# Four clears of the accumulator in flight at most, and the rows of x for the second stage fetched one per step

## The chip, the core and the metric

The kernel is one program on one core of a Trainium2 chip. The metric is the device time of one execution in microseconds (us). The engines named below are PE (matrix multiply), DVE (vector), ACT (scalar functions), POOL (GpSimd; here it issues the indirect DMAs and, in the second stage, normalizes) and SP (here it only issues plain DMAs). Each takes its own instructions in order and meets the others at semaphores. DMAs issued by SP, ACT and POOL run on the same 16 DMA engines.

## What is computed

One layer of a message-passing network over 50,000 atoms and 50,000 edges with 256 features, then a layer norm over 2x + m:

```python
h = x @ W_in2f
Wij = ssp(rbf @ Wf1 + bf1) @ Wf2 + bf2      # ssp(z) = softplus(z) - log 2
Wij = Wij * dist_cut
x_ij = h[idx_j] * Wij
m = jax.ops.segment_sum(x_ij, idx_i, num_segments=n_atoms)
m = ssp(m @ Wo1 + bo1) @ Wo2 + bo2
return x + m
...
x = _layernorm(x + _L0_gnn_ref(...), axis=-1)
```

## The kernel before

**Stage one** goes over the edges in G = 98 groups of 512 (R = 4 rows of 128 edges in each). POOL gathers the rows of x that the edges name (line 341, four gathers of 128 rows a group, into the ring `xg` of XRING = 11 groups). PE turns them (420), multiplies by W_in2f (409) and makes the filter from `attr`; ACT and DVE evaluate softplus and split each operand into a high and a low part; PE multiplies the message by Wo1 at once, sums edges of a group that go to the same atom (495), and ACT copies the result into `sums`, a ring of RING = 12 groups. POOL adds `sums` into the accumulator `acc` in HBM with four indirect scatter-adds a group (354). Every engine runs its stages with lags: in step s, PE turns and filters group s, multiplies group s-1, and so on to group s-3; DVE's `compare` (744), last in its step, handles group s-2.

**The accumulator is cleared first.** `acc` has 50,512 rows of 256 floats. SP fills them with `fill` (a constant row) in 195 DMAs of 256 KB (line 271) and three more for the rest (279), all on one semaphore `cleared`. The first scatter waits for all of them. SP's order is written out by hand: eight clears (EARLY_CLEARS), a wait until group 0 is gathered, clears up to number 36 (FIRST_CLEARS), the three of the rest, and then for n = 2 to 98: `load_attr(n)` (250, two DMAs, waits for a freed buffer through `al_sb`), `load_src(n-1)` (255, waits for `compare` of group n-3 through `same_ready`), and 16 more clears (CLEARS_A_STEP) as long as there are any. The last 15 stand behind `load_src(10)`.

**POOL's order** is written out too: 23 groups are gathered first (AHEAD; from group 11 on each waits until PE has turned group g-11), then come the scatters of one group and three or four gathers in turn. The first scatter of a group waits until those of the group before have landed (`added`).

**Stage two** goes over the atoms in 98 groups of 512: SP fetches rows of `acc` (`fetch_m`, 293) and of x (`fetch_x`, 299), PE turns and multiplies by Wo2, and POOL normalizes (379 to 385); SP stores (304). The x rows use the ring `xg` again, 11 groups. The first 11 x fetches stand in SP's order behind all loads of stage one, in a burst; each waits until PE has turned the last edge group in its slot (`xt_ps`). The first `fetch_m` waits until all scatters have landed.

Of the kernel before, what the change touches and what calls it, by code (L numbers as in the profile page):

```python
# [44 lines left out]
P = 128  # L45
R = 4
RING = 12
XRING = 11
ARING = 2
SRING = 2  # L50
AHEAD = 23
EARLY_CLEARS = 8
FIRST_CLEARS = 36
CLEARS_A_STEP = 16
LOG2 = 0.6931471805599453
LN_MAX = 40.0
# [17 lines left out]
def wait(eng, sem, value):  # L74

    if isinstance(value, int) and value <= 0:
        return
    eng.wait_ge(sem, value)  # L78


def build(nc, t, out):
    N, D = t["x"].shape
    E = N
    G, A = t["edge_attr_64"].shape[:2]
# [5 lines left out]
    def group(n):  # L90
        return Group(n, n % 2, n // 2 + 1, ROWS if n < G - 1 else TAIL)

    def run(*stages, before={}):

        for s in range(G + max(lag for _, lag in stages)):
            if s in before:
                before[s]()  # L100
            for stage, lag in stages:
                if 0 <= s - lag < G:
                    stage(group(s - lag))

    acc = nc.dram_tensor("acc", [N + R * P, D], F32, kind="Internal").ap()

    with ExitStack() as ctx:
        def sb(name, shape, dt=F32):
            return ctx.enter_context(nc.sbuf_tensor(name, shape, dt))

        def sem(name):
            return ctx.enter_context(nc.semaphore(name))
# [31 lines left out]
        CLEAR = 2  # L144
        fill = sb("fill", [P, CLEAR, D])
# [26 lines left out]
        x_in = xg  # L172
# [6 lines left out]

        dve_own = sem("dve_own")  # L180
        dst_in, src_in, wgt_in, tab_made = sem("dst_in"), sem("src_in"), sem("wgt_in"), sem("tab_made")
        bo1_in, fill_made, cleared = sem("bo1_in"), sem("fill_made"), sem("cleared")
        made = sem("made")
        bo2_zero, bo2_in = sem("bo2_zero"), sem("bo2_in")
        wf1_in, w_in_in, b_in, wf2_in, wo1_in, wo2_in = (sem(n) for n in ("wf1_in", "w_in_in", "b_in", "wf2_in", "wo1_in", "wo2_in"))
# [6 lines left out]
        xg_in = [sem(f"xg_in{u}") for u in range(XRING)]  # L192
# [4 lines left out]
        xt_ps = sem("xt_ps")  # L197
# [16 lines left out]
        x_got = [sem(f"x_got{u}") for u in range(XRING)]  # L214
# [3 lines left out]
        res_sb, mean_sb = sem("res_sb"), sem("mean_sb")  # L218
# [4 lines left out]

        block = ctx.enter_context(nc.Block())

        CLEARS = N // P // CLEAR
        TABLES = 1 + R
        assert N // P % CLEAR == 0
        CLEAR_REST = len(range(CLEARS * CLEAR * P, N + R * P, CLEAR * P))

        def rows_of(ap, g):

            return ap[bass.ds(g.n * ROWS, g.rows)]
# [9 lines left out]
        @block.sync  # L243
        def _(sp):

            def load_attr(n):
                g, u = group(n), n % ARING
                wait(sp, al_sb, n - ARING + 1)
                for k in range(2):
                    sp.dma_start(attr[k * A:(k + 1) * A, u], t["edge_attr_64"][n]).then_inc(attr_in[u], 16)  # L250

            def load_src(n):
                g, u = group(n), n % SRING
                wait(sp, same_ready, (n - SRING + 1) * R)
                sp.dma_start(srcb[:, u], t["src_rows"][n].partition_broadcast(P)).then_inc(srcb_in[u], 16)

            sp.dma_start(dst_t[:].rearrange("p r g -> p (r g)"), t["dst"].rearrange("p r g -> p (r g)")).then_inc(dst_in, 16)
            load_attr(0)
            sp.dma_start(bo1, t["L0_gnn_bo1"].partition_broadcast(P)).then_inc(bo1_in, 16)
            sp.dma_start(src_i.rearrange("p r g -> p (r g)"), t["src"].rearrange("p r g -> p (r g)")).then_inc(src_in, 16)  # L260
            sp.dma_start(wgt_t[:].rearrange("p r g -> p (r g)"), t["edge_weight1"].rearrange("p r g -> p (r g)")).then_inc(wgt_in, 16)
            load_attr(1)
            load_src(0)

            sp.wait_ge(fill_made, 1)
            clears = 0

            def clear_to(count):
                nonlocal clears
                for c in range(clears, min(count, CLEARS)):  # L270
                    sp.dma_start(acc[c * CLEAR * P:(c + 1) * CLEAR * P, :].rearrange("(p k) d -> p (k d)", k=CLEAR), fill[:, 0:CLEAR].rearrange("p k d -> p (k d)")).then_inc(cleared, 16)
                clears = max(clears, min(count, CLEARS))

            clear_to(EARLY_CLEARS)
            sp.wait_ge(xg_in[0], 16 * R)
            clear_to(FIRST_CLEARS)
            for a in range(CLEARS * CLEAR * P, N + R * P, CLEAR * P):
                b = min(a + CLEAR * P, N + R * P)
                sp.dma_start(acc[a:b, :].rearrange("(p k) d -> p (k d)", k=CLEAR), fill[0:(b - a) // CLEAR].rearrange("p k d -> p (k d)")).then_inc(cleared, 16)
            for n in range(2, G + 1):  # L280
                if n < G:
                    load_attr(n)
                load_src(n - 1)
                clear_to(FIRST_CLEARS + (n - 1) * CLEARS_A_STEP)
            assert clears == CLEARS
            wait(sp, al_sb, G - ARING + 1)
            sp.dma_start(wo2, t["L0_gnn_Wo2"]).then_inc(wo2_in, 16)

            def fetch_m(g):
                if g.n == 0:  # L290
                    sp.wait_ge(added, 16 * R * G)
                wait(sp, mt_ps, (g.n - MRING + 1) * H)
                sp.dma_start(m_in[0:g.p, g.n % MRING].rearrange("p r d -> p (r d)"), rows_of(acc, g).rearrange("(p r) d -> p (r d)", r=R)).then_inc(m_got[g.n % MRING], 16)

            def fetch_x(g):
                if g.n < XRING:
                    sp.wait_ge(xt_ps, 2 * max(n + 1 for n in range(G) if n % XRING == g.xs))
                wait(sp, res_sb, g.n - XRING + 1)
                sp.dma_start(x_in[0:g.p, g.xs].rearrange("p r d -> p (r d)"), rows_of(t["x"], g).rearrange("(p r) d -> p (r d)", r=R)).then_inc(x_got[g.xs], 16)

            def store(g):
                u = g.n % NRING
                sp.wait_ge(norm_sb, g.n + 1)
                sp.dma_start(rows_of(out, g).rearrange("(p r) d -> p (r d)", r=R), normed[0:g.p, u].rearrange("p r d -> p (r d)")).then_inc(stored[u], 16)

            for n in range(G - XRING, G):
                fetch_x(group(n % XRING))
            for s in range(G + 8):
                if s < G:
                    fetch_m(group(s))  # L310
                if 8 <= s:
                    store(group(s - 8))
                if XRING <= s - 1 < G:
                    fetch_x(group(s - 1))

            for u in range(NRING):
                sp.wait_ge(stored[u], 16 * len(range(u, G, NRING)))
# [3 lines left out]
        def _(pool):  # L321
# [23 lines left out]
            def scatter(r):  # L345
                def stage(g):
                    if r == 0:
                        if g.n == 0:
                            pool.wait_ge(cleared, 16 * (CLEARS + CLEAR_REST))
                        pool.wait_ge(src_ready, g.n + 1)  # L350
                        wait(pool, added, g.n * R * 16)
                    if r % 2 == 0:
                        pool.wait_ge(y_sb, g.n * 2 + r // 2 + 1)
                    pool.indirect_dma_start(acc, bass.IndirectOffsetOnAxis(ap=src_ix[g.slot][0:g.p, r:r + 1], axis=0),  # L354
                                            sums[0:g.p, g.slot, r], None, compute_op=ALU.add).then_inc(added, 16)
                return stage
# [526 lines left out]
```

## Time and profile before

| | |
|---|---|
| median of 3 runs | 1865.61 us (1861.05 to 1866.87) |
| the profiled execution | 1858.28 us, span 1856.5 us |
| granted PE clock, mean of the span | 0.972 |
| busy share of the span | PE 91%, PEld 83%, DVE 80%, ACT 80%, POOL 78% |
| DMA | 363.47 MB, 196 GB/s over the span |
| queue q1 (SP's DMAs) | 257.75 MB |
| queue q0 (POOL's DMAs) | 102.45 MB |

A busy share is a mean over stages that have different limits; the 40 slices of the page show three of them: a start with idle engines and full DMA, the long stage one with DMA at six or seven tenths, and stage two with DMA nearly full. POOL's share leaves out the time in which it issues, some 0.3 us in front of each indirect DMA.

### The profile page before, as it was taken

To read this page: it belongs to the slowest core of one execution; us is meant where nothing else is said; L and a number is where in the kernel's file an instruction comes from. 1 tells how busy PE (TensorE), PEld (TensorE's weight loads), DVE (VectorE), ACT (ScalarE), POOL (GpSimd) and SP (SyncE) were. 2 spreads that over 40 slices of the span, in tenths; PEclk is the share of its full clock that TensorE was granted. 3 is DMA by queue.
4 is the path that set the end of the run, shared out by engine and by line. 5 is a ranking of instruction groups with operands and counts; after the bars stand their busy time and mean duration, and the time that the engine had idled before them with its cause. 6 is when DMAs were issued, how large, how long until landed. Compare 5 with 4: busy or idle time off the path is not lost. (4 is left out here: it accounts for less than half of the span.)

```text
span 1856.5 us, 36676 instructions
## 1 busy us (share of the span) xinstructions
PE 1697.3 (91%) x11376; PEld 1532.2 (83%) x11376; DVE 1489.3 (80%) x3750; ACT 1492.9 (80%) x2945; POOL 1441.4 (78%) x1385
## 2 busy tenths in 40 slices
PE   3499899999999999999999998889976999999995
PEld 2378788888888888888888887778866999999995
DVE  2477788787888888888888786777765999999996
ACT  2477788778888788888888786776756999999996
POOL 7422488888887888878888888888754999999997
PEclk9699999999999999999999998999998999999998
DMA  9799866656566665666665666665675999999994
GB/s 354 251 356 372 266 123 112 126 112 125 115 125 122 112 123 114 124 125 112 125 120 116 119 122 113 114 118 108 116 185 170 333 363 362 360 360 364 357 366 174
DMA packets 177341, 363.47 MB, mean 196 GB/s; under 512 B 25622, under 2 KB 76264, under 8 KB 177148
## 3 DMA queue, kind: packets, MB, share of 16 engines
q1 hardware_dynamic: 101128, 257.75, 39.8%
q0 software_dynamic: 75136, 102.45, 32.4%
q8 instruction: 93, 1.52, 0.3%
q10 hardware_dynamic: 884, 0.92, 0.2%
q14 instruction: 100, 0.82, 0.1%
HBM read 206.90 MB, written 154.12 MB: 194 GB/s over the span
## 5 line engine op out<-in xcount | busy, mean ns | idle before, releaser
L354 POOL DMA_INDIRECT acc<-sums,src_ix x392 | 637.2, 1626 | 141.6 <-issue 116.0
L341 POOL DMA_INDIRECT xg<-in_x,dst_t x392 | 401.4, 1024 | 215.6 <-issue 114.6
L780 DVE SCALAR_TENSOR_TENSOR m_l<-pair,wgt_t,m_h 128x256 fp32r<-128x256 f32 x392 | 171.6, 479 | 230.5 <-ACT m_h L621 206.6
L385 POOL TENSOR_SCALAR sums<-sums,neg_mean,rstd 128x256 f32<-128x256 f32 x392 | 283.2, 733 | 10.2
L495 PE MATMUL pair<-m_h,same 128*128 128x256 f32 (+1 forms) x980 | 244.8, 285 | 30.4 <-ACT sums L628 21.9
L621 ACT ACTIVATE m_h<-pair,wgt_t 128x256 fp32r<-128x256 f32 x392 | 165.0, 475 | 99.5 <-PE pair L409 57.6
L495 PE MATMUL pair<-m_l,same 128*128 128x256 f32 (+1 forms) x980 | 241.8, 281 | 0.0
L409 PE MATMUL pair<-wo_h,msg_h 128*128 128x256 f32 (+1 forms) x784 | 230.9, 295 | 6.0 <-DVE m_l L780 5.2
L495 PEld LDWEIGHTS pair<-m_h,same 128*128 128x128 f32 (+1 forms) x980 | 185.1, 189 | 52.2 <-issue 34.9
L576 ACT ACTIVATE zs<-pair,bf 128x512 f32<-128x512 f32 x196 | 124.1, 685 | 125.8 <-PE pair L433 99.5
L409 PE MATMUL pair<-wo_h,msg_l 128*128 128x256 f32 (+1 forms) x784 | 222.0, 283 | 0.0
L409 PE MATMUL pair<-wo_l,msg_h 128*128 128x256 f32 (+1 forms) x784 | 221.5, 283 | 0.0
L527 PE MATMUL pair<-w_in_l,ssp_h 128*128 128x256 f32 (+1 forms) x784 | 220.6, 281 | 0.0
L527 PE MATMUL pair<-w_in_h,ssp_l 128*128 128x256 f32 (+1 forms) x784 | 220.5, 281 | 0.0
L527 PE MATMUL pair<-w_in_h,ssp_h 128*128 128x256 f32 (+1 forms) x784 | 220.3, 281 | 0.0
L744 DVE SCALAR_TENSOR_TENSOR same<-srcb,src_t,later 128x512 fp32r<-128x512 int32 (+3 forms) x392 | 192.8, 546 | 0.0
L495 PEld LDWEIGHTS pair<-m_l,same 128*128 128x128 f32 (+1 forms) x980 | 185.0, 189 | 6.7
L763 DVE SCALAR_TENSOR_TENSOR msg<-pair,bias_w,h_sb 128x512 f32<-128x512 f32 x196 | 146.1, 746 | 54.7 <-remote 37.6
L673 DVE TENSOR_TENSOR ssp_l<-ssp,ssp_h 128x512 fp32r<-128x512 f32 (+1 forms) x245 | 186.2, 793 | 4.5 <-ACT ssp_h L653 2.8
L409 PE MATMUL pair<-ssp_h,wf_h 128*128 128x512 f32 x392 | 164.4, 419 | 25.8 <-DVE msg L763 25.8
L409 PE MATMUL pair<-x_h,w_in_h 128*128 128x512 f32 x392 | 155.5, 397 | 18.7 <-issue 18.6
L662 ACT ACTIVATE srcb<-sums,neg_mean 128x256 f32<-128x256 f32 x294 | 158.9, 636 | 3.1 <-DVE neg_mean L835 3.1
(97 smaller groups left out, 5249.8 us busy)
## 6 DMA issues: line engine op xcount, KB each, us to landing
acc<-fill SPq DMA_DIRECT2D x197, 256.0 KB
xg<-in_x SPq DMA_DIRECT2D x97, 512.0 KB, 6.4
sums<-acc SPq DMA_DIRECT2D x97, 512.0 KB, 6.8
out<-sums SPq DMA_DIRECT2D x97, 512.0 KB, 4.7
attr<-in_edge_attr SPq DMA_DIRECT2D x196, 128.0 KB
srcb<-in_src_rows SPq DMA_DIRECT2D x98, 256.0 KB
xg<-in_x,dst_t POOLq DMA_INDIRECT x392
acc<-sums,src_ix POOLq DMA_INDIRECT x392
```

The costliest lines, as they stand in the source:

```text
L341: pool.indirect_dma_start(xg[0:g.p, g.xs, r], None, t["x"], bass.IndirectOffsetOnAxis(ap=dst_t[0:g.p, r, g.n:g.n + 1], axis=0)).then_inc(x ...
L354: pool.indirect_dma_start(acc, bass.IndirectOffsetOnAxis(ap=src_ix[g.slot][0:g.p, r:r + 1], axis=0), sums[0:g.p, g.slot, r], None, compute ...
L385: last = pool.tensor_scalar(normed[0:g.p, g.n % NRING, r], res[0:g.p, u, r], neg_mean[0:g.p, u, r:r + 1], rstd[0:g.p, u, r:r + 1], ALU.add ...
L409: last = pe.matmul(o, a, b, start=n == 0, stop=n == len(terms) - 1)
L495: last = pe.matmul(o, same[0:g.p, g.par, FROM[a] + b - a, 0:g.p], m[0:g.p, a], start=a == 0 and m is m_h, stop=a == b and m is m_l)
L527: last = pe.matmul(o, sp2[:, g.par, h, r, 0:g.p], w[:, h, :], start=False, stop=h == H - 1 and sp2 is ssp2_l)
L621: act.activation(m_h[0:g.p, r], bank[6][0:g.p, k * D:(k + 1) * D], ACT.Copy, scale=col(wgt_t, r, g)).then_inc(mh_sb, 1)
L662: last = act.activation(squares[0:g.p, r], res[0:g.p, u, r], ACT.Square, bias=neg_mean[0:g.p, u, r:r + 1], accum_out=square[0:g.p, u, r:r ...
L673: dve.tensor_tensor(out_, whole, high.bitcast(F32), ALU.subtract).then_inc(done, count)
L744: dve.scalar_tensor_tensor(out=same[0:g.p, g.par, FROM[a]:FROM[a] + R - a, 0:g.p], in0=sources[:, a:R], scalar=col(src_t, a, g), in1=later ...
L763: dve.scalar_tensor_tensor(out=msg[:, m], in0=bank[5][:], scalar=bias_w[:, m:m + 1], in1=h_sb[:, m], op0=ALU.add, op1=ALU.mult).then_inc(m ...
L780: dve.scalar_tensor_tensor(out=m_l[0:g.p, r], in0=bank[6][0:g.p, k * D:(k + 1) * D], scalar=col(wgt_t, r, g), in1=m_h[0:g.p, r].bitcast(F3 ...
```

## The change

Clears now use four semaphores in turn, and before clear c is issued SP waits until clear c-4 has landed. The wait for group 0 after eight clears is gone. The rest of the rows is no longer cleared early: it is part of the count, which becomes 198, so that the last two clears stand one step later, behind `load_src(11)`. POOL's first scatter waits on the four semaphores. `fetch_x` is called once per step for n = 89 to 98, behind that step's `load_src`, and once behind the loop; before, all 11 stood behind the loop.

```diff
-EARLY_CLEARS = 8
 FIRST_CLEARS = 36
+IN_FLIGHT = 4
...
-        bo1_in, fill_made, cleared = sem("bo1_in"), sem("fill_made"), sem("cleared")
+        bo1_in, fill_made = sem("bo1_in"), sem("fill_made")
+        cleared = [sem(f"cleared{u}") for u in range(IN_FLIGHT)]
...
-        CLEARS = N // P // CLEAR
+        CLEARS = -(-(N + R * P) // (P * CLEAR))
...
                 for c in range(clears, min(count, CLEARS)):
-                    sp.dma_start(acc[c * CLEAR * P:(c + 1) * CLEAR * P, :]...).then_inc(cleared, 16)
+                    a, b = c * CLEAR * P, min((c + 1) * CLEAR * P, N + R * P)
+                    wait(sp, cleared[c % IN_FLIGHT], c // IN_FLIGHT * 16)
+                    sp.dma_start(acc[a:b, :]...).then_inc(cleared[c % IN_FLIGHT], 16)
                 clears = max(clears, min(count, CLEARS))
 
-            clear_to(EARLY_CLEARS)
-            sp.wait_ge(xg_in[0], 16 * R)
             clear_to(FIRST_CLEARS)
-            for a in range(CLEARS * CLEAR * P, N + R * P, CLEAR * P):
...
                 clear_to(FIRST_CLEARS + (n - 1) * CLEARS_A_STEP)
+                if G - XRING <= n - 2:
+                    fetch_x(group((n - 2) % XRING))
...
-            for n in range(G - XRING, G):
+            for n in range(G - 1, G):
                 fetch_x(group(n % XRING))
...
                         if g.n == 0:
-                            pool.wait_ge(cleared, 16 * (CLEARS + CLEAR_REST))
+                            for u in range(IN_FLIGHT):
+                                pool.wait_ge(cleared[u], 16 * len(range(u, CLEARS, IN_FLIGHT)))
```

SP at the start of the program, before (`acc<-fill` is a clear, `fill_made` says that the constant row is there, `xg_in0` that group 0 is gathered):

```order
8 L271 DMA acc<-fill 128x512 [waits fill_made]
9 L271 DMA acc<-fill 128x512 x7
10 L271 DMA acc<-fill 128x512 [waits xg_in0]
11 L271 DMA acc<-fill 128x512 x27
12 L279 DMA acc<-fill 128x512 x2
13 L279 DMA acc<-fill 40x512
14 L250 DMA attr<-in_edge_attr 64x512 [waits al_sb]
```

and in the changed kernel, where rows 10 to 41 are 32 clears with a wait each:

```order
8 L273 DMA acc<-fill 128x512 [waits fill_made]
9 L273 DMA acc<-fill 128x512 x3
10 L273 DMA acc<-fill 128x512 [waits cleared0]
11 L273 DMA acc<-fill 128x512 [waits cleared1]
...
41 L273 DMA acc<-fill 128x512 [waits cleared3]
42 L250 DMA attr<-in_edge_attr 64x512 [waits al_sb]
```

Each clear from the fifth on has moved behind the landing of the one four places ahead, and the wait for group 0 has gone.

SP at the end of the clears, before (the last 15, then two steps' loads) and in the changed kernel:

```order
52 L255 DMA srcb<-in_src_rows 128x512 [waits same_ready]
53 L271 DMA acc<-fill 128x512 x15
54 L250 DMA attr<-in_edge_attr 64x512 [waits al_sb]
55 L250 DMA attr<-in_edge_attr 64x512
56 L255 DMA srcb<-in_src_rows 128x512 [waits same_ready]
```

```order
232 L250 DMA attr<-in_edge_attr 64x512 [waits al_sb]
233 L250 DMA attr<-in_edge_attr 64x512
234 L255 DMA srcb<-in_src_rows 128x512 [waits same_ready]
235 L273 DMA acc<-fill 128x512 [waits cleared0]
236 L273 DMA acc<-fill 40x512 [waits cleared1]
```

The row with 40 partitions, once at the start, now ends the clears, behind the `load_src` that waits for one group more.

SP at the end of stage one, before and in the changed kernel (`xg<-in_x` is a fetch of x, 512 KB):

```order
311 L255 DMA srcb<-in_src_rows 128x512 [waits same_ready] x2
312 L287 DMA attr<-in_L_gnn_Wo 128x512 [waits al_sb]
313 L299 DMA xg<-in_x 128x1024 [waits xt_ps] x11
314 L293 DMA sums<-acc 128x1024 [waits added]
```

```order
499 L255 DMA srcb<-in_src_rows 128x512 [waits same_ready]
500 L282 DMA xg<-in_x 128x1024 [waits xt_ps]
501 L255 DMA srcb<-in_src_rows 128x512 [waits same_ready]
502 L282 DMA xg<-in_x 128x1024 [waits xt_ps]
503 L293 DMA attr<-in_L_gnn_Wo 128x512 [waits al_sb]
504 L282 DMA xg<-in_x 128x1024 [waits xt_ps]
505 L299 DMA sums<-acc 128x1024 [waits added]
```

Ten of the eleven fetches have moved up, one into each of ten steps; the last two of these are the rows 500 and 502.

## Rows read from the trace of the kernel before

**Rows 1.** The chain that ended last, at the turn of the stages: start us, us, what

```profile
1400.35 3.18 DMA sums<-acc
```

**Rows 2.** Busy time by stretch: stretch, length, busy us of each engine, PEclk, DMA share, GB/s

```profile
0.00:60.00 60.00, 15.61 (x50) 11.89 (x50) 10.29 (x28) 12.85 (x21) 44.86 (x58) 0.85 0.95 340
60.00:212.00 152.00, 128.95 (x786) 111.95 (x787) 111.91 (x256) 109.31 (x211) 44.78 (x49) 0.95 0.94 339
212.00:1397.00 1185.00, 1121.78 (x7014) 992.96 (x7012) 944.68 (x2192) 941.16 (x1831) 949.51 (x692) 0.98 0.63 121
```

**Rows 3.** Waits from 212 to 1397 us: who waited for what, us in total, times, longest

```profile
POOL acc L354 <- issue: 116.0, 347, 3.2
...
POOL xg L341 <- issue: 90.2, 296, 0.3
```

**Rows 4.** SP's DMA issues in order of time, stage two: start us, us, issue

```profile
1449.02 0.34 SPq L304 DMA_DIRECT2D out<-sums  x1
...
1453.39 0.34 SPq L304 DMA_DIRECT2D out<-sums  x1
```

**Rows 5.** The same view of SP over the first 210 us

```profile
7.73 34.94 SPq L271 DMA_DIRECT2D acc<-fill  x36
...
51.89 19.60 SPq L271 DMA_DIRECT2D acc<-fill  x16
71.49 0.46 SPq L250 DMA_DIRECT2D attr<-in_edge_attr  x2
81.31 0.34 SPq L255 DMA_DIRECT2D srcb<-in_src_rows  x1
...
96.00 13.02 SPq L271 DMA_DIRECT2D acc<-fill  x16
109.06 1.32 SPq L250 DMA_DIRECT2D attr<-in_edge_attr  x2
110.43 0.59 SPq L255 DMA_DIRECT2D srcb<-in_src_rows  x1
...
207.85 0.58 SPq L255 DMA_DIRECT2D srcb<-in_src_rows  x1
```

**Rows 6.** All engines in order of time, with the idle time before and its releaser

```profile
27.23 0.16 DVE L694 TENSOR_TENSOR bias_w<-bf,pair 128x2 f32<-128x2 f32 x1 [14.13 <-issue]
...
37.03 0.40 PE L409 MATMUL pair<-ssp_h,wf_l 128*128 128x512 f32 x1
...
71.73 0.75 DVE L763 SCALAR_TENSOR_TENSOR msg<-pair,bias_w,h_sb 128x512 f32<-128x512 f32 x1 [37.64 <-remote]
...
211.91 1.64 POOL L354 DMA_INDIRECT acc<-sums,src_ix  x1 [0.30 <-issue]
```

**Rows 7.** DMA, 0 to 19.5 us: queue, packets, MB, share; and the clears issued

```profile
q1 hardware_dynamic: 2040, 3.36, 53.6%
...
acc<-fill SPq DMA_DIRECT2D x17, 256.0 KB
```

**Rows 8.** The same view, 0 to 45 us

```profile
q1 hardware_dynamic: 6286, 11.09, 67.9%
...
acc<-fill SPq DMA_DIRECT2D x37, 256.0 KB
```

**Rows 9.** DMA, SP's queue from 85 to 206 us

```profile
q1 hardware_dynamic: 22155, 40.11, 89.4%
```

**Rows 10.** SP's own waits, stage two: for the landing of the last store (336 KB)

```profile
SPq L317 <- DMA out<-sums: 2.5, 1, 2.5
```

**Rows 11.** The page's DMA issues: count, KB each, median us from issue to landing

```profile
out<-sums SPq DMA_DIRECT2D x97, 512.0 KB, 4.7
```

**Rows 12.** SP in order of time: the burst of x fetches

```profile
1356.75 6.17 SPq L299 DMA_DIRECT2D xg<-in_x  x11
```

**Rows 13.** POOL in order of time: first scatters of two groups behind the burst

```profile
1371.10 1.55 POOL L354 DMA_INDIRECT acc<-sums,src_ix  x1 [7.07 <-DMA acc<-sums,src_ix]
...
1381.42 1.55 POOL L354 DMA_INDIRECT acc<-sums,src_ix  x1 [3.18 <-issue]
```

More of the change, by code:

```diff
@@ L224, in build @@
         block = ctx.enter_context(nc.Block())
-        CLEARS = N // P // CLEAR
+        CLEARS = -(-(N + R * P) // (P * CLEAR))
         TABLES = 1 + R
-        assert N // P % CLEAR == 0
-        CLEAR_REST = len(range(CLEARS * CLEAR * P, N + R * P, CLEAR * P))
+        assert (N + R * P) % CLEAR == 0
         def rows_of(ap, g):
@@ L270, in clear_to, with fetch_x @@
                 for c in range(clears, min(count, CLEARS)):
-                    sp.dma_start(acc[c * CLEAR * P:(c + 1) * CLEAR * P, :].rearrange("(p k) d -> p (k d)", k=CLEAR), fill[:, 0:CLEAR].rearrange("p k d -> p (k d)")).then_inc(cleared, 16)
+                    a, b = c * CLEAR * P, min((c + 1) * CLEAR * P, N + R * P)
+                    wait(sp, cleared[c % IN_FLIGHT], c // IN_FLIGHT * 16)
+                    sp.dma_start(acc[a:b, :].rearrange("(p k) d -> p (k d)", k=CLEAR),
+                                 fill[0:(b - a) // CLEAR].rearrange("p k d -> p (k d)")).then_inc(cleared[c % IN_FLIGHT], 16)
                 clears = max(clears, min(count, CLEARS))
-            clear_to(EARLY_CLEARS)
-            sp.wait_ge(xg_in[0], 16 * R)
             clear_to(FIRST_CLEARS)
-            for a in range(CLEARS * CLEAR * P, N + R * P, CLEAR * P):
-                b = min(a + CLEAR * P, N + R * P)
-                sp.dma_start(acc[a:b, :].rearrange("(p k) d -> p (k d)", k=CLEAR), fill[0:(b - a) // CLEAR].rearrange("p k d -> p (k d)")).then_inc(cleared, 16)
+            def fetch_x(g):
+                if g.n < XRING:
+                    sp.wait_ge(xt_ps, 2 * max(n + 1 for n in range(G) if n % XRING == g.xs))
+                wait(sp, res_sb, g.n - XRING + 1)
+                sp.dma_start(x_in[0:g.p, g.xs].rearrange("p r d -> p (r d)"), rows_of(t["x"], g).rearrange("(p r) d -> p (r d)", r=R)).then_inc(x_got[g.xs], 16)
             for n in range(2, G + 1):
@@ L293, in fetch_m @@
                 sp.dma_start(m_in[0:g.p, g.n % MRING].rearrange("p r d -> p (r d)"), rows_of(acc, g).rearrange("(p r) d -> p (r d)", r=R)).then_inc(m_got[g.n % MRING], 16)
[L295 to L299, printed above, removed]
             def store(g):
```

## The prediction

> **What bounds the kernel now.** I read the chain of waits first. It comes, through stage two, to the first fetch of `acc` at 1400.35 us [rows 1], which waits for the last scatter. So the program is two parts laid end to end, and the reader has to ask what sets the pace of each.
>
> Stage two runs at one group in 4.37 us (the stores at 1449.02 and 1453.39 [rows 4]), 98 of them in 428 us. The change alters neither its work nor the eleven x groups that stand ready when it begins. I leave it as it is; what is won or lost before 1400 us arrives at the end unchanged.
>
> Stage one after 212 us is POOL's. In the 1185 us from 212 to 1397 POOL is busy 949.5 us [rows 2], and the gaps in front of its DMAs, which it spends on issuing, are 116.0 + 90.2 = 206 us [rows 3]. Together that is 1156 of 1185 us: POOL is committed for 97.5% of the stretch, and PE with 1122 us has more room. So the end of stage one is the time of the first scatter plus 1185 us. Only an earlier first scatter (211.91 us, [rows 6]) or a shorter tail moves it.
>
> What sets the first scatter? It needs all clears, and in POOL's order it stands behind the gather of group 22, which waits until PE has turned group 11. Both hang on the step count of the pipeline. SP's `load_src` rows are its clock: that of step 2 is issued at 81.31, that of step 11 at 207.85 us [rows 5]. Nine steps in 126.5 us are 14.06 us each; the first two took 81 us. That is odd, and the next view says why: in the first 60 us PE works 15.6 us and DVE 10.3 us, while DMA runs at 340 GB/s [rows 2]. In order of time [rows 6], DVE stands 14.13 us until 27.23 us, and then 37.64 us more until `msg` at 71.73 us. The last product that `msg` needs was started on PE at 37.03 us and lasted 0.40 us (its other input is ACT's copy of a product that PE had made still earlier). DVE waits for work that PE did long ago. At the same time SP needs 19.60 us for 16 clears, while from 96 us on it needs 13.02 us [rows 5]. The congestion ends at 71.5 us, when that burst ends: `load_attr` is issued at 71.49 us in 0.46 us for two DMAs, and DVE starts 0.24 us later.
>
> **The cap, at the start.** By 19.5 us SP had issued 17 clears of 0.262 MB behind 1.52 MB of loads (sizes in the code), 5.98 MB, and its queue had moved 3.36 MB [rows 7]: 2.6 MB, ten clears' worth, stood in the queue, and this is when the first long idle time of DVE had begun. By 45 us it was 37 x 0.262 + 1.52 = 11.22 MB issued and 11.09 moved [rows 8]. Clears got 9.57 MB in the 37.3 us since 7.73 us, or 1.02 us each. A cap of four in flight makes a backlog of ten impossible.
>
> How much do four carry? The last store, 336 KB with nothing beside it, landed 0.34 us of issue plus 2.5 us [rows 10] after it was issued. Taken at the pace of stage two (three times 0.524 MB in 4.37 us, 360 GB/s [rows 4]), its bytes need 0.95 us, so about 1.9 us are fixed, and a lone clear takes 1.9 + 0.73 = 2.6 us. Four in 2.6 us are 403 GB/s, above what the queue moved, clears and loads together: 40.11 MB in 121 us, 331 GB/s, from 85 to 206 us [rows 9]. So I take the cap as wide enough; if landing takes longer under load, it isn't (below).
>
> Then the start is bounded by bytes. The 52 clears ahead of `load_src(2)` take 52 x 1.02 = 53.1 us, its other loads (0.52 MB at the same rate) 2.0 us: 7.73 + 55.1 = 63 us instead of 81.3. Would PE be there? It had worked through step 1 by 37.4 us [rows 6]; `attr(2)` is issued at 7.73 + 36 x 1.02 = 44.5 us, lands some 2.6 us later, and one whole step of 14 us behind it ends at 61 us, so yes, narrowly. **Term 1: -17 us**, from -19 to 0 (the stall stays).
>
> **The cap, from step 2 to step 11.** SP issued 16 clears in 13.02 us [rows 5] and was never far ahead; with waits for landings the DMA engines will run dry now and then, when SP is at its other loads. I allow 2.5% of 126.5 us. **Term 2: +3 us**, from 0 to +35 (a landing of 4 us, below). The added wait holds up what is queued behind it on SP, `load_attr` and `load_src` of the next step, and through them ACT, DVE and PE; this is why the term counts in full.
>
> **The last two clears** move behind `load_src(11)`, issued at 207.85 us. Issue and landing are 0.3 + 0.7 + 2.6 us, so they would have landed at 211.5 us, against the first scatter at 211.91, set by the gathers. **Term 3: 0**, up to +2 us where the landing is slower.
>
> **The x fetches.** Before, eleven went out from 1356.75 us on in 6.17 us [rows 12], 5.6 MB, and POOL's next group of scatters waited 7.07 us for the landing of the one before, where the following group waited 3.18 us [rows 13]. Spread out, that wait is 3.2 us too: -3.9 us. The tail behind it is four scatters and one landing for each group, so the shift goes through. In their new places, ten fetches of 1.46 us of transfer each fall into steps where POOL has three or four gathers between two groups, some 4 us that cover a landing of 3.2 us; a collision costs under 1 us, and not each collides. +1 us. The new waits (`xt_ps` of the group two steps back) are met when `load_src` ahead of them is. **Term 4: -3 us**, from -4 to +3.
>
> **The sum.** -17 + 3 + 0 - 3 = -17 us. The profiled execution, 1858.28 us, would take 1841.3 us. It lies 7.3 us under the median of 1865.61 us; against that median the sum gives 1848.6 us, which is my number.
>
> **Rivals.** *The stall isn't a matter of depth.* From 51.89 to 71.49 us the clears went out at 1.2 us each, hardly over what the queue moved, so there was no deep backlog then, and still DVE and ACT stood until 71.7 us. If the cause is gathers and clears side by side, or SP's issuing as such, a cap changes nothing at the start. Then term 1 falls away: 0 to 3 - 3 = 0, with the range of the terms -6 to +3, 1860 to 1868 us, about 1864 us. For it: POOL gathers nearly without a pause in the same 60 us (busy 44.9 us [rows 2], plus a gap at each). Against it: DVE's first long wait falls together with the deepest backlog. The Trainium skill speaks for this rival: the page "DMA: Bandwidth & Descriptors", section "Queues, rings and completion order", says that each DMA engine serves the queues that have work in turn, packet by packet, so a long queue of one does not keep the others out. By that rule term 1 would be about 0 as far as it is about data; the trace agrees in that POOL's gathers went on at their pace, and speaks against it in that SP's congestion and everybody's ended at the same moment.
>
> *The cap starves the clears (the slower side).* The median store of 512 KB took 4.7 us to land in full traffic [rows 11]. If a clear takes L us under load, one goes out every L/4 us, and a step is 16 x L/4 + 1.9 us for SP's other loads (1.32 + 0.59 us [rows 5]). It overtakes the old 14.06 us at L = 3.04 us; the nine steps eat the whole gain of terms 1 and 4 (20 us) at L = 3.6 us, and from there the kernel is slower. At 4.0 us a step is 17.9 us, +35 us over nine, and the sum -17 + 35 - 3 = +15 us: 1881 us. At 4.7 us it is 20.7 us a step, +60, and the start 8 us later, about 1913 us. Against it: in a full queue the waiting is the engines' being busy, which costs nothing.
>
> *The start is quicker still.* If term 2 is 0 and the start is bounded by bytes at the best rate, terms reach -19 and -4: 1843 us or a little less, 1841.
>
> **How the numbers follow.** The forecast (with its quicker end) has 0.55, the unchanged stall 0.24, starving 0.18, and 0.03 is for anything else. The forecast's own range is 1841 to 1858 us. For eight in ten I go from 1840 up to 1882 us, which takes in the second rival and the starving case at its middle price. About 0.3%, 5.6 us, is what a measurement of this kernel can tell from no change. Faster by over that (below 1860 us): the forecast and a few hundredths of the rivals, 0.60. Same (1860 to 1871 us): most of the unchanged stall and the mild part of starving, 0.24. Slower: 0.16.
>
> **What would show it.** Term 1: SP's third `srcb` issue near 63 us instead of 81.31, and no idle time over 5 us on DVE and ACT between 20 and 70 us; if it is still near 80 us, the first rival holds. Term 2: steps of 14 to 14.5 us between the third and the twelfth `srcb`; steps of 17 us, with SP waiting on landings of clears and DMA under 330 GB/s, mean starving. Term 3: the first scatter within 5 us of the twelfth `srcb`. Term 4: no wait of POOL over 3.5 us in the last four groups. And the stretch from the first scatter to the last must still be close to 1185 us; if it grows by what the start gained, PE and not POOL was the bound, and the forecast is wrong there.

## The result: slower by 1.6%

The changed kernel takes 1893.82 us (median of 4 runs, 1892.17 to 1898.87) against 1865.21 us (4 runs, 1861.05 to 1866.87) for the kernel before: a ratio of 1.0161, interval 1.0136 to 1.0187, so 28.6 us more. The forecast was 1848.6 us and its range ended at 1882. The profiled execution took 1898.87 us with a span of 1897.1 us, 40.6 us more than the profiled execution of before; where it went is read from these two, each against its own span.

The turn of the stages, in SP's issues in order of time (start us, us). The first fetch of `acc` has moved from 1400.35 [rows 1] to 1439.39 us, 39.0 of the 40.6 us. Stage two keeps its pace: 457.7 us from there to the end of the span, 456.2 before.

```profile
1439.39 18.68 SPq L299 DMA_DIRECT2D sums<-acc  x8
```

Busy time by stretch, the three stretches of [rows 2] cut at the new first scatter (columns as there: length, busy us of PE, PEld, DVE, ACT, POOL, granted clock, DMA share, GB/s):

```profile
0.00:60.00 60.00, 14.67 (x50) 11.20 (x50) 10.42 (x28) 14.68 (x24) 44.78 (x58) 0.78 0.92 314
60.00:243.00 183.00, 141.76 (x818) 123.37 (x819) 117.81 (x267) 112.21 (x217) 45.31 (x48) 0.89 0.84 293
243.00:1436.00 1193.00, 1115.70 (x6982) 993.87 (x6980) 939.87 (x2182) 939.47 (x1822) 948.42 (x692) 0.97 0.64 119
```

The stretch before the first scatter has grown by 31 us, and there the DMA engines' share has fallen from 0.94 to 0.84 and their rate from 339 to 293 GB/s. The long stretch has grown by 8 us.

Both of these shares are means over two different things. In either kernel some 10 us at the end of the stall at the start have little DMA (share 0.30 before, 0.08 from 77 to 87 us in the changed kernel): SP waits 9.3 and 9.7 us there for `compare` before it may issue more. Here is that hole in the kernel before, then what follows it, before and changed:

```profile
72.00:81.00 9.00, 8.37 (x39) 7.03 (x40) 8.36 (x18) 6.25 (x14) 3.71 (x5) 0.76 0.30 90
82.00:212.00 130.00, 119.58 (x744) 104.10 (x744) 102.31 (x235) 99.80 (x194) 36.94 (x40) 1.00 1.01 366
```

```profile
87.00:235.00 148.00, 126.15 (x738) 110.48 (x737) 102.23 (x235) 100.00 (x194) 36.21 (x39) 0.93 0.91 318
```

So in the nine steps alone the share went from 1.01 to 0.91 and the rate from 366 to 318 GB/s.

SP's first 240 us, the view of [rows 5]:

```profile
8.12 43.60 SPq L273 DMA_DIRECT2D acc<-fill  x36
...
55.98 20.31 SPq L273 DMA_DIRECT2D acc<-fill  x16
77.00 0.02 SPq L250 DMA_DIRECT2D attr<-in_edge_attr  x2
86.77 0.34 SPq L255 DMA_DIRECT2D srcb<-in_src_rows  x1
...
152.28 15.08 SPq L273 DMA_DIRECT2D acc<-fill  x16
167.41 1.23 SPq L250 DMA_DIRECT2D attr<-in_edge_attr  x2
168.68 0.60 SPq L255 DMA_DIRECT2D srcb<-in_src_rows  x1
...
234.55 0.60 SPq L255 DMA_DIRECT2D srcb<-in_src_rows  x1
235.19 0.97 SPq L273 DMA_DIRECT2D acc<-fill  x2
```

The third `srcb` issue stands at 86.77 us (81.31 before), the twelfth at 234.55 (207.85): the nine steps between take 147.8 us where they took 126.5. The nine blocks of 16 clears behind it take 13.4 to 15.5 us (mean 14.4); before, the eight full ones took 11.5 to 13.0 us (mean 12.1). What SP waited for in this stretch, 86 to 236 us (us in total, times, longest); the kernel before has no such wait:

```profile
SPq L273 <- DMA acc<-fill: 57.8, 96, 3.8
```

At the start, DVE in order of time, the view of [rows 6]: the second long idle time is there still, and longer. (The first is shorter, 7.12 us where it was 14.13, since the work in front of it came earlier; the two together went from 51.8 to 57.2 us.)

```profile
77.19 0.75 DVE L764 SCALAR_TENSOR_TENSOR msg<-pair,bias_w,h_sb 128x512 f32<-128x512 f32 x1 [50.12 <-remote]
```

POOL in order of time, at the first scatter and in the last groups, as in [rows 6] and [rows 13]:

```profile
235.23 0.95 POOL L341 DMA_INDIRECT xg<-in_x,dst_t  x1 [0.30 <-issue]
243.01 1.63 POOL L355 DMA_INDIRECT acc<-sums,src_ix  x1 [6.83 <-DMA acc<-fill]
...
1409.43 1.76 POOL L355 DMA_INDIRECT acc<-sums,src_ix  x1 [3.87 <-DVE src_ix L756]
...
1420.13 1.75 POOL L355 DMA_INDIRECT acc<-sums,src_ix  x1 [2.98 <-DMA acc<-sums,src_ix]
...
1430.50 1.50 POOL L355 DMA_INDIRECT acc<-sums,src_ix  x1 [3.04 <-DMA acc<-sums,src_ix]
```

So the 39.0 us are: +5.5 to the third `srcb` issue, +21.2 in the nine steps, +4.4 between the last of these and the first scatter (from 4.1 to 8.5 us, now ended by the landing of the last clears, 6.83 us of idle time where before it was 0.30), and +7.9 from the first scatter to the landing of the last.

### The profile page after: what moved, and what is told of

It is laid out like the page before. It is cut to its first block and busy times, and to the rows that moved or that the text cites. A ratio compares the mean times of both kernels' runs of the same rounds, so it can differ in the third digit from the quotient of the medians.

```text
span 1897.1 us, 36678 instructions
## 1 busy us (share of the span) xinstructions
PE 1704.5 (90%) x11376; PEld 1545.0 (81%) x11376; DVE 1490.6 (79%) x3750; ACT 1496.0 (79%) x2945; POOL 1440.8 (76%) x1385
## 5 line engine op out<-in xcount | busy, mean ns | idle before, releaser
L622 ACT ACTIVATE m_h<-pair,wgt_t 128x256 fp32r<-128x256 f32 x392 | 165.0, 474 | 116.1 <-PE pair L410 87.2
L410 PE MATMUL pair<-wo_h,msg_h 128*128 128x256 f32 (+1 forms) x784 | 232.5, 297 | 3.9 <-DVE m_l L781 3.9
L421 PE MATMUL pair<-ident,xg 128*128 128x128 f32 (+1 forms) x784 | 124.2, 284 | 58.6 <-DMA xg<-in_x,dst_t 58.1
```

The lines of the kernel that those rows point to most:

```text
L410: last = pe.matmul(o, a, b, start=n == 0, stop=n == len(terms) - 1)
L622: act.activation(m_h[0:g.p, r], bank[6][0:g.p, k * D:(k + 1) * D], ACT.Copy, scale=col(wgt_t, r, g)).then_inc(mh_sb, 1)
```

## The experiments

Each is one edit. T is the issue of the third `srcb`, N the nine steps from it to the twelfth, F the first scatter, S the stretch from F to the first fetch of `acc`. All in us, from the profiled execution of each. The last column is the ratio of the median to that of the kernel before timed beside it, with its interval; a kernel with a single execution has its time in us instead, and the first row the median.

| kernel | T | N | F | S | time |
|---|---|---|---|---|---|
| before | 81.3 | 126.5 | 211.9 | 1188.4 | 1865.2 |
| before, again | 83.8 | 127.8 | 217.7 | 1191.3 | 1868.5 |
| changed | 86.8 | 147.8 | 243.0 | 1196.4 | 1.0161 (1.0136 to 1.0187) |
| changed, again | 87.2 | 144.8 | 237.9 | 1191.1 | 1887.4 |
| cap of 4 alone | 85.7 | 144.2 | 236.2 | 1187.8 | 1.0096 (1.0064 to 1.0128) |
| x fetches alone | 86.0 | 126.9 | 216.2 | 1198.4 | 1.0015 (0.9991 to 1.0039) |
| changed, cap of 8 | 86.9 | 127.6 | 221.6 | 1197.9 | 1.0043 (1.0026 to 1.0061) |
| cap of 2 | 97.3 | 203.8 | 306.3 | 1213.2 | 1978.8 |
| before, gathers paced | 56.8 | 150.1 | 210.7 | 1194.0 | 0.9998 (0.9976 to 1.0019) |
| the same, again | 54.2 | 155.4 | 214.9 | 1190.8 | 1865.0 |
| before, clears late | 38.1 | 192.2 | 232.5 | 1203.8 | 1.0175 (1.0137 to 1.0212) |
| before, lead of 4 | 54.1 | 126.6 | 185.2 | 1230.3 | 1874.5 |
| before, x fetches later | 55.8 | 131.1 | 192.8 | 1209.6 | 0.9981 (0.9959 to 1.0002) |
| the same, again | 81.5 | 126.7 | 213.9 | 1188.6 | 1863.4 |

### The two parts apart

The cap without the spread fetches, an edit of the changed kernel:

```diff
-                if G - XRING <= n - 2:
-                    fetch_x(group((n - 2) % XRING))
...
-            for n in range(G - 1, G):
+            for n in range(G - XRING, G):
                 fetch_x(group(n % XRING))
```

> The changed kernel with its eleven x fetches put back behind the loop, in a burst: the cap of four and the four semaphores alone. Theory A (the cap starves the clears: in the changed kernel's trace the nine steps from the third to the twelfth srcb issue take 147.8 us instead of 126.5, and the first scatter comes 31 us late): the first scatter stays near 243 us and the time is about 1893 us or a little more, with POOL's 7 us wait at the burst back. Rival B (the x fetches, which now land among the last gathers, cost the most): the time falls by 10 us or more, to 1883 us or less.

1882.80 us against 1865.14: +17.7 us. That is 11.0 us under the changed kernel and just within what the rival had asked for (1883 us or less); still the cap is the larger part. SP's wait for clears between 85 and 230 us is the one of the changed kernel, and the nine steps are 144.2 us:

```profile
SPq L273 <- DMA acc<-fill: 56.6, 100, 3.1
```

The fetches without the cap, the kernel before with the same three lines the other way round:

> The kernel before with its x fetches moved one into each of the last ten steps, nothing else. Theory A: the first scatter at 212 us as before; the tail gains 3 to 4 us at the burst and loses at most 1 us elsewhere, so 1862 us, within 0.3% of before. Rival B (x fetches delay gathers and with them PE, the stretch from first to last scatter grew by 8 us in the changed kernel): 1870 to 1875 us.

1869.18 against 1865.14 us, ratio 1.0015, with an interval that holds no change, and a hair short of the rival's 1870. The cap alone and the fetches alone make +17.7 and +4.0 us, the two together +28.6; the 7 us between are not accounted for, and a second execution of the changed kernel (below) took 23.2 us more than the kernel before beside it. For the fetches only the profile speaks. The scatters of the groups 80 to 93 took 182.2 us, against 170.7 in the kernel before; the four traces with spread fetches have 182.1 to 184.0 us there, those without have 170.7 to 175.6 (the lead of 4 apart, which has more gathers there). What follows, groups 94 to 96, takes 33.2 us instead of 37.0. Net the scatters lose some 8 us in this pair. The kernel before happens to be the fastest of its kind here: on the means of the four traces with spread fetches and of the six without that are named at term 4 below, the groups 80 to 93 lose 10.0 us, and the net is some 6. The burst's wait [rows 13] that I meant to save is the small half. Waits in that stretch, before (1183.8 to 1354.5 us):

```profile
PE pair L420 <- DMA xg<-in_x,dst_t: 15.5, 6, 8.5
POOL acc L354 <- issue: 15.3, 49, 0.6
```

and with the fetches spread (1190.3 to 1372.5 us):

```profile
PE pair L422 <- DMA xg<-in_x,dst_t: 32.2, 5, 11.9
POOL acc L356 <- issue: 21.2, 42, 2.9
...
POOL acc L356 <- DVE src_ix L757: 4.2, 2, 2.5
```

One such place in order of time, SP and then POOL: the 0.5 MB of x go out at 1323.31 us, just ahead of the last scatter of a group at 1325.90, whose landing then isn't covered by the three gathers behind it.

```profile
1322.93 0.33 SPq L255 DMA_DIRECT2D srcb<-in_src_rows  x1
1323.31 0.43 SPq L284 DMA_DIRECT2D xg<-in_x  x1
1323.78 1.14 SPq L250 DMA_DIRECT2D attr<-in_edge_attr  x2
```

```profile
1325.90 1.55 POOL L356 DMA_INDIRECT acc<-sums,src_ix  x1 [0.30 <-issue]
...
1332.60 1.63 POOL L356 DMA_INDIRECT acc<-sums,src_ix  x1 [1.28 <-issue]
```

About half of the 11.5 us is in front of scatters in this way (21.2 against 15.3 us), 4.2 us is POOL's waiting for `compare`, which stands behind PE; PE waits twice as long for gathers. How these two feed each other I have not taken apart, and no run has the fetches at another place within the step.

### How many clears in flight

The changed kernel with one number changed, IN_FLIGHT = 8:

> The changed kernel with eight clears in flight on eight semaphores. Theory A: twice the depth at the landing time seen with four (16 clears in 14.4 us, so 3.6 us for one with four in flight) is more than DMA can carry, so the cap no longer binds and steps are back at 14 us; first scatter near 214 us, time 1864 to 1868 us. Rival C (it is the wait instructions on SP or the semaphores that cost, not the depth): steps stay near 16.4 us, time about 1893 us.

1874.14 us, some 6 us over what was expected; the fetches alone have 4.0 us of the 9.0 over the kernel before, and the rest is not accounted for. The nine steps are back at 127.6 us, and SP's wait for clears between 86 and 214 us is

```profile
SPq L273 <- DMA acc<-fill: 2.7, 8, 0.7
```

The other side is two in flight, with the fetches in a burst as in the cap alone:

> Two clears in flight, x fetches in the burst as before: a gauge of how long one clear takes to land. By my prediction's figure (2.6 us alone, 1.9 of it fixed) 16 clears take 16 x 2.6 / 2 = 21 us, a step 23 us, nine steps 207 us and the kernel about 1925 us. Theory A' (a clear lands in 3.6 us even when only four are in flight, because the fixed part is about 2.9 us beside gathers and loads): 16 clears take 26 to 29 us, nine steps 250 us or more, 1970 us.

One execution, 1978.79 us, 54 us over the first figure, though the steps came out by it (203.8 us for 207, which alone would have made 1946 of 1865). Against the profile of the kernel before, 16 us are in front of the third `srcb` issue, 77 in the nine steps, 1 behind them, and 25 behind the first scatter; the expectation had counted the nine steps alone. SP in order of time:

```profile
119.13 0.58 SPq L255 DMA_DIRECT2D srcb<-in_src_rows  x1
119.76 21.21 SPq L273 DMA_DIRECT2D acc<-fill  x16
141.01 1.12 SPq L250 DMA_DIRECT2D attr<-in_edge_attr  x2
142.18 0.58 SPq L255 DMA_DIRECT2D srcb<-in_src_rows  x1
```

The nine blocks of 16 clears took 19.98 to 21.70 us, mean 20.8. With two in flight a block is 16/2 landings, so a clear lands in 20.8 / 8 = 2.60 us, the 2.6 us of the prediction. With four in flight a block was 13.4 to 15.5 us (mean 14.4), or 14.4 / 4 = 3.6 us a landing. With eight it was 11.6 to 12.4 us (mean 12.0), as without a cap (12.1), and SP hardly waited. So the landing is not a constant, as the prediction had it: it grows with what else is in flight. These figures come from the pace of SP's issues; the landings' own records in the traces, counted from the end of an issue, have means of 2.4, 3.6 and 4.7 us for two, four and eight. One clear went out every 1.30 us with two in flight, every 0.90 with four and every 0.75 with eight.

### What the first scatter waits for: the bytes, and the rate at which they move

One view puts the kernels in a row: the DMA engines from 0 to the twelfth `srcb` issue. Some 70.5 MB go by until then (70.4 to 71.3 MB; 58 MB of SP's, 11.6 MB of gathers; 67 MB with the shorter lead, which gathers less), 71.9 MB up to the first scatter of the kernel before. The mean rates differ: before (0 to 212 us), changed (0 to 235), later fetches in their first execution (0 to 187), a row of each:

```profile
DMA packets 38012, 71.92 MB, mean 339 GB/s; under 512 B 5633, under 2 KB 6275, under 8 KB 37996
```

```profile
DMA packets 37356, 70.75 MB, mean 301 GB/s; under 512 B 5537, under 2 KB 6179, under 8 KB 37340
```

```profile
DMA packets 37269, 70.51 MB, mean 377 GB/s; under 512 B 5516, under 2 KB 6158, under 8 KB 37254
```

and 308 GB/s for the cap of 4 alone, 328 for the cap of 8, 237 for that of 2. A mean rate is bytes over time, so 70.75 MB / 301 GB/s = 235 us explains nothing by itself; what the rows say is that the bytes stay the same from kernel to kernel and the rate does not. The share of 0.94 [rows 2] looks like a full stretch, but it isn't one: the 9 us at 90 GB/s are in it, and an execution without the stall moved the same bytes in 187 us, 21 us sooner. So there was something to win at the start, if not by this change, while a cap that holds the rate down over nine steps is paid in full.

### The stall at the start

The gathers paced, in the kernel before: POOL gathers group g only when PE has turned g/2 - 1 groups, where before the first 11 groups went without a wait.

```diff
-                        wait(pool, xt_ps, (g.n - XRING + 1) * 2)
+                        wait(pool, xt_ps, max(g.n - XRING + 1, min(g.n // 2 - 1, XRING)) * 2)
```

> The kernel before, but POOL's first gathers are paced: group g waits until PE has turned group g/2 - 2 (so four groups go at once and then two per step), instead of eleven groups at once; the 23 groups ahead of the first scatter are the same. Theory D (the stall of the first 70 us comes from POOL gathering without a pause beside clears without a pause): DVE and ACT don't stand over 5 us between 27 and 70 us, the third srcb issue comes at 60 us or earlier instead of 81, the first scatter 15 to 20 us earlier, time 1845 to 1852 us. Rival E (it comes from SP issuing clears, whatever POOL does): third srcb issue near 80 us still, time 1862 to 1868 us.

> The kernel of e4 (POOL's first gathers paced) once more. If pacing itself removes the stall, the third srcb issue is at 57 us again, within 3 us, and steps four to seven take 19 to 20 us again; if e4 was luck, it is as variable as the kernel before.

The stall is gone in both profiled executions (third `srcb` at 56.8 and 54.2 us), with all clears uncapped and SP's queue as deep as ever. And the time is unchanged, ratio 0.9998: the gathers that were put off are made up for two groups at a time in the next steps, which last 18.8 to 20.3 us. The first scatter is where it was. The expectation was right on the stall and wrong on the time (1845 to 1852 us).

Then no clears at all until 11 groups are gathered, and 25 a step from there:

```diff
-            clear_to(EARLY_CLEARS)
-            sp.wait_ge(xg_in[0], 16 * R)
-            clear_to(FIRST_CLEARS)
...
-                clear_to(FIRST_CLEARS + (n - 1) * CLEARS_A_STEP)
+                if n == 4:
+                    sp.wait_ge(xg_in[XRING - 1], 16 * R)
...
+                clear_to(max(n - 3, 0) * 25)
```

> The kernel before with no clear before POOL has gathered its first eleven groups (about 60 us), then 25 clears a step instead of 16. Theory D' (the stall needs gathers and clears side by side, since pacing the gathers in e4 brought step 2 to 56.8 us): no engine stands over 5 us between 27 and 60 us, the third srcb issue comes before 50 us and the fourth before 62 us; then steps of 25 x 0.73 + 1.9 = 20 us; first scatter near 220 us, time about 1872 us. Rival H (gathers alone stall the others): the third srcb issue comes at 75 us or later, time above 1890 us.

```profile
0.00:60.00 60.00, 42.39 (x222) 36.02 (x223) 39.47 (x93) 39.91 (x73) 44.91 (x57) 1.00 0.56 161
60.00:230.00 170.00, 109.15 (x600) 96.13 (x599) 81.58 (x190) 80.79 (x157) 43.96 (x48) 0.80 0.99 362
```

PE works 42 us of the first 60 instead of 16, POOL gathers as before: in this trace gathers without clears go with no stall, as clears beside paced gathers do above. It is one trace, and the stall can be missing by itself (below, in an execution on the same chip), so this side is less firm than the pacing, which was seen twice, each time beside executions that had the stall. DMA ran at 161 GB/s in those 60 us, and what it didn't move had to follow: the first scatter came 21 us late, the stretch behind it took 15 us more, and the time was 1896.97 us, where 1872 had been expected.

A lead of four groups at most (AHEAD 15, a gather waits until PE is within four groups):

```diff
-AHEAD = 23
+AHEAD = 15
...
-                        wait(pool, xt_ps, (g.n - XRING + 1) * 2)
+                        wait(pool, xt_ps, max(g.n - XRING + 1, min(g.n - 3, XRING + 1)) * 2)
```

> The kernel before with POOL never more than four groups ahead of PE until the clears are done (four gathers a step beside 16 clears, 15 groups gathered before the first scatter instead of 23). Theory D': no stall and no long step at all: third srcb issue near 57 us as in e4, then steps of 14 us instead of e4's 19 to 20 us, twelfth near 184 us, first scatter near 188 us. The eight groups that are not gathered ahead cost POOL 32 x 1.25 = 40 us later, so the time is about 1880 us. Rival I (e4's steps of 19 to 20 us come from the clears, not from eight gathers a step): steps four to seven stay at 19 us or more, first scatter later than 200 us.

No stall (54.1 us) and the steps at 13.1 to 14.7 us; first scatter 185.2 us, 27 us sooner, but with eight groups more still to gather among the scatters. 32 gathers of 0.96 + 0.3 us are 40 us; S is 42 us longer; 1874.53 us in its one execution.

### What an earlier first scatter is worth

The kernel before with each x fetch behind a `fetch_m` of stage two:

```diff
-            for n in range(G - XRING, G):
-                fetch_x(group(n % XRING))
...
+                if s < XRING:
+                    fetch_x(group(s))
```

> The kernel before with the eleven x fetches neither in a burst nor spread over stage one: each stands behind the fetch of acc for the same group, after the last scatter has landed. Theory F (in the last groups of stage one POOL's path includes the landing of scatters, and any half megabyte that SP fetches there lengthens it: 7.07 us instead of 3.18 at the burst, 11.5 us over groups 80 to 94 in e2): the wait at the burst falls to 3.2 us, groups 80 to 94 take 171 us as before, stage one ends 4 us earlier; stage two starts with 5.8 MB more to fetch in a stretch of 25 us in which DMA moved 176 GB/s, so it loses 0 to 4 us. Time 1861 to 1865 us. Rival G (the start of stage two is bound by its own fetches): it loses more than it gains, 1868 us or more.

> The kernel of e5b once more. Theory J: the third srcb issue can be anywhere from 55 to 87 us. Theory K (something in the program, such as where its code lies, decides): 56 us again.

1861.92 against 1864.63 us, ratio 0.9981 (0.9959 to 1.0002), not told from no change. What the two profiles of this one program show is worth more. In the first the stall wasn't there, in the second it was; nothing in the program differs. The first scatter of each:

```profile
192.79 1.64 POOL L354 DMA_INDIRECT acc<-sums,src_ix  x1 [0.30 <-issue]
```

```profile
213.88 1.64 POOL L354 DMA_INDIRECT acc<-sums,src_ix  x1 [0.30 <-issue]
```

and the first fetch of `acc`:

```profile
1402.41 0.33 SPq L293 DMA_DIRECT2D sums<-acc  x1
```

```profile
1402.46 0.33 SPq L293 DMA_DIRECT2D sums<-acc  x1
```

21 us sooner at 200 us, and nothing left of it at 1400. Busy times from 300 to 700 us, the early one and then the late one:

```profile
300.00:700.00 400.00, 400.00 (x2536) 358.06 (x2535) 342.59 (x792) 344.33 (x670) 312.50 (x229) 1.00 0.63 118
```

```profile
300.00:700.00 400.00, 397.90 (x2520) 355.96 (x2519) 339.70 (x786) 341.31 (x665) 326.90 (x239) 1.00 0.63 121
```

In the early execution PE never stops, and POOL gets through 229 DMAs where the other gets through 239. PE's step and POOL's group are both 12.6 us there, over 50 groups, where POOL otherwise takes 12.17 us. With equal periods they don't drift past one another: SP's loads, released at the end of PE's step, go out right at a group's last scatter each time (502.17 and 514.78 us against 501.99 and 514.60), and the landing is then covered no more:

```profile
501.99 1.56 POOL L354 DMA_INDIRECT acc<-sums,src_ix  x1 [0.30 <-issue]
...
508.25 1.62 POOL L354 DMA_INDIRECT acc<-sums,src_ix  x1 [0.83 <-issue]
...
514.60 1.57 POOL L354 DMA_INDIRECT acc<-sums,src_ix  x1 [0.30 <-issue]
...
521.14 1.62 POOL L354 DMA_INDIRECT acc<-sums,src_ix  x1 [1.11 <-issue]
```

Over the whole trace it looks the same: in each of the first 51 groups of the early execution a `srcb` load is issued between 0.5 us before and 1.4 us behind the start of the group's last scatter, while in the late one the distance drifts from -6 to +6 us and round again.

The late clears of above show the same state (groups 20 to 60 at 12.5 us, PE busy 300.00 of 300 us from 500 to 800), and so does the cap of two, whose first scatter came 94 us late: 12.57 us a group over its first 50, its loads at the same place, S of 1213.2 us.

```profile
350.00:750.00 400.00, 400.00 (x2543) 358.21 (x2542) 343.54 (x792) 345.11 (x670) 312.70 (x230) 1.00 0.63 118
```

So it isn't a return to a fixed end; it is a state that costs 0.4 us a group, into which the early execution fell. Three of the thirteen traces with a lead of 23 groups have it. That the loads are what uncovers the landing is read from where they stand; no run moved them. Nor was PE's room even: of the 400 us from 300 to 700 PE is busy 392 in the kernel before and 395 in the changed one.

### Before and changed once more

> The kernel before, once more, unchanged. In e5b, whose first 1340 us are instruction for instruction those of the kernel before, the third srcb issue came at 55.8 us instead of 81.3, though the time stayed the same. Theory J (the stall of the start is a matter of the single execution, and stage one makes up for it later): a second profile of the kernel before may show the third srcb issue anywhere from 55 to 87 us, and the stretch from first to last scatter is the shorter the later the first scatter is (1188 us at 212, 1210 at 193). Theory K (it is fixed by the program): 81 us again, within 5 us.

> The changed kernel once more. The cap's effect must not depend on the start: whatever the third srcb issue is (86.8 us the first time), the nine steps behind it take 144 to 150 us, against 126 to 131 us without the cap.

The nine steps repeat nearly, 127.8 and 144.8 us, 17.0 apart where the first pair is 21.2; so does SP's wait for clears in the changed kernel, 57.9 us in 99 waits. The wait for the last clears in front of the first scatter was 2.72 us this time, not 6.83. The first scatter varies by some 6 us between executions of one kernel (211.9 and 217.7; 243.0 and 237.9), so of the four terms above only that of the nine steps is firm, as 17 to 21 us (17.7 with the cap alone), and the 5.5 and the 4.4 us are not.

## Why the prediction was wrong, point by point

**What bounds the kernel.** Two parts laid end to end, right: stage two kept its pace, and 39.0 of 40.6 us of the spans are ahead of it. That the end of stage one is the first scatter plus 1185 us held for some later starts (1188 with the cap alone, 24 us late) and failed for an earlier one, 1209.6 us, and for two later ones, 1203.8 (late clears) and 1213.2 us (cap of two). The prediction named the first case in its last sentence. Its PE "has more room" was a mean over the stretch: from 300 to 700 us PE is busy 392 of 400 us. Even a right term 1 would have been given back in that early execution.

**Term 1, -17 us, was +5.5.** This is the failed step on the gaining side: that the stall comes from the depth of SP's queue. With the cap 8 clears and the loads had been issued by 19.5 us, 3.62 MB, and 3.06 MB of them moved: 0.56 MB stood in the queue instead of 2.6, and DVE's second idle time went from 37.64 to 50.12 us. (The working gave 81.3 - 62.8 = 18.5 us; where the 17 comes from is not said.) The first rival ("the stall isn't a matter of depth") held, and its row was the right one to weigh: clears at 1.2 us each up to 71.5 us are no backlog. The coincidence of deepest backlog and DVE's first wait was weaker evidence than its continuation long after. The Trainium skill's rule that I set against my own term (page "DMA: Bandwidth & Descriptors", section "Queues, rings and completion order": the engines serve the queues in turn) agrees with all of this as far as it goes, but does not tell what the stall is. The runs say when it comes: gathers without a wait beside clears. With the gathers paced it's gone (twice), in the one trace with the clears held back too; and it can be missing with both there (55.8 us). What in it holds ACT and DVE back no run shows.

**Term 2, +3 us, was +21.2 (+17.7 in the kernel with the cap alone).** This is the failed step that decided the sign: "four in 2.6 us are 403 GB/s, so I take the cap as wide enough". The 2.6 us was right for two clears in flight (2.60 measured). It was used for four beside gathers and loads, where it is 3.6 us, so that four carry 291 GB/s; 20.8 us a block at two, 14.4 at four and 12.0 at eight, where the wait is gone, leave no room for the new waits or semaphores as such. The starving rival had the formula: 16 x 3.6 / 4 + 1.9 = 16.3 us a step, measured 16.4 (the 3.6 is taken from these same steps). It put break-even of the whole at 3.6 us, given a gain of 20 us; without that gain 3.04 us was the point from which the cap costs. Its argument against itself, that "in a full queue the waiting is the engines' being busy", was wrong: their share in the nine steps fell from 1.01 to 0.91. Both rivals came in together, and my range had no case for both at once: term 1 gone and term 2 at +20 (a landing of 3.6 us) give +20 - 3 = +17 us, 1882.6 us, its upper end before anything else goes wrong.

**Term 3, 0 us.** The prediction allowed up to +2. The first scatter did wait for the last two clears, with 6.83 us of idle time (2.72 in the second trace), which made 4.4 us; from the end of their issue (235.19 + 0.97) to the first scatter it was 6.85 us (4.3 in the second trace), not 2.6.

**Term 4, -3 us, was about +6** (S has a mean of 1196.0 us in the four traces with spread fetches, and of 1190.2 in six without: before and paced gathers twice each, the cap alone, the later fetches' second). The saving was there: the 7.07 us are gone, the last three groups take 33 to 34 us instead of 37. The price was mis-sized: "a collision costs under 1 us, and not each collides". It was 10.0 us in 14 groups on these means (11.5 in the one pair), 1.0 us for each of ten fetches. I put it down to where the fetch stands, right behind `load_src`, released by the same step that releases everything else; no run shows that.

**The signs to look for** did their work: third `srcb` near 80 us, steps of 17 us, SP waiting for clears, DMA under 330 GB/s, and the first scatter more than 5 us behind the twelfth `srcb` all point to the rivals.

## What to carry to other kernels

When a stretch has the DMA engines at 0.94, sum its bytes first, then cut it finer: the stretch here was 130 us at 366 GB/s behind a hole of 9 us at 90. Where the rate is full, take any edit that makes an issuer wait for landings as a loss until its width is shown. The width of a cap is (in flight x bytes) / landing, and the landing must be the one at that depth and beside that traffic, not of a lone transfer; with a margin of a few tenths of a microsecond, take the slower side as the forecast. And a start that comes earlier is worth what the engines behind it can use: look at the second busiest one (PE at 1122 of 1185 us, and at 392 of 400 from 300 to 700 us) before carrying the gain through to the end.

## What I had not expected of the hardware

- A clear of 256 KB lands in 2.6 us with two in flight and in 3.6 us with four, beside the same gathers and loads; with eight the clears go out every 0.75 us, as with no cap.
- At the start ACT is let go at 34.24, 44.74, 56.03, 67.23 and 77.17 us in the changed kernel, 9.9 to 11.3 us apart, each time for a product that PE had finished long before; this happened with POOL's gathers unchecked beside SP's clears, in nine of the ten profiled executions with both (T between 81 and 97 us), and not in the tenth (55.8). The lower layer of it stays open.
- Two engines whose periods come to the same number (12.6 us) can stay in an unlucky phase for 50 groups, at 0.4 us each.
